# A state-space layer with a mixture of experts on one Trainium2 core: a new order for the first stage, with the third group's sine arguments made by GpSimd

## The chip, the cores and the metric

The kernel runs on one core of one Trainium2 chip. Its time is the device time of one launch, in microseconds. Five engines run their own instruction queues and meet at semaphores: TensorE (PE), VectorE (DVE), ScalarE (ACT), GpSimd (POOL) and SyncE (SP), which only issues DMAs. All data are float32.

## What is computed

```python
h = layernorm(x)                          # x: 2 x 2048 x 128
u = h @ in_W.T + in_b                     # along the sequence, per channel (128)
A = -exp(log_A_real) + 1j * A_imag        # 128 channels x 32 modes
K = exp(A * dt * arange(2048))
k = 2 * einsum('hn,hnl->hl', C * (exp(A * dt) - 1) / A, K).real
y = causal_convolution(u, k) + u * D_skip
y = gelu(y); z = y @ glu_W.T + glu_b; y = a * sigmoid(g)    # a, g: halves of z
x = x + (y @ out_W.T + out_b + h)
h = layernorm(x)                          # then 14 routed experts (top 2) and 2 shared ones
x = x + (moe(h) + h)
```

## The kernel before

The convolution is cut into 16 chunks of 128 positions per sequence. Within a chunk it is a product with a Toeplitz matrix of the first 128 values of k; from chunk to chunk a state of 32 complex modes per channel is carried. Both come from one table v1: for position s and mode n, exp(-|a|s) times sine and cosine of the mode's angle. The 128 channels are four groups of 32 (g = 0 to 3, 1024 columns each). This **first stage** is the span up to about 104 us; the gated unit, the routing and the loop over expert blocks follow and are the same in both kernels.

What the first stage does, and who does it:

- SP loads x, writes the small parameters `ab` to DRAM and reads them back broadcast to all partitions, one load of 1 MB a group (`abb[g]`, L394; groups 0 and 1 in `area`, 2 and 3 in `xn`). Later it loads the Toeplitz matrices of each group (`hank[g]`, L412) once the impulse response of that group is stored (`kp_out`), and for groups 2 and 3 once all of v1 is there.
- PE turns x by 512 columns at a time (`turn_x`, eight units, banks 0 and 1), ScalarE copies the turned block (`evict_xnT`, L1025), PE projects it (`project_in`, L1282, banks 2 to 7, then 2 and 3 again), and VectorE evicts the result (`evict_u`, L698, four operations a unit). The eviction scales by the reversed reciprocal roots `rstdr`, which one small product puts into bank 0 and VectorE copies (`reversed_roots`, L676).
- `table_args(g)` (VectorE, L685 to L690, four operations of 128x1024) brings the angle to within half a turn: round by adding and taking away a large constant, subtract, and clear the sign for the cosine's argument. `magnitude(g)` (ScalarE, L1034) makes the exponentials, `sines(g)` (ScalarE, L1039 and L1040) sine and cosine. `products(g)` (VectorE, L361, two of 128x1024) multiplies them into v1.
- PE makes the chunk states `states(g)` (L1293, into bank g), transposes the tables `turn_tables(g)` (L1306), which ScalarE copies into v2 (`evict_v2`, L1059), and multiplies them into the impulse response, `impulse(g)` (L1319), which ScalarE copies into `ksb` and stores (`evict_k`, L1065 to L1069). `ksb` shares its memory with the turned x and is cleared by a GpSimd memset first (L550).
- GpSimd makes the small coefficients `q1` and `q2` in a chain of 128x32 operations (L502 to L547). PE spreads them into banks 6 and 7 (L1337 to L1340), from where ScalarE copies `lw` and VectorE `cbig` (L724).
- VectorE weighs the states (L744 to L746) and runs the recurrence over the chunks (L756 to L761). ScalarE and VectorE copy its results into `s_bd` (L1105, L769). PE multiplies u with the Toeplitz matrices (L1361), then reads the states (L1370), which closes the convolution.

The order on each engine is written out by hand, and every queue is strictly in order. Before the change VectorE runs: arguments 0 and 1, eight evictions, products 0, cbig, arguments 2, products 1, arguments 3, products 2, products 3. `link(...)` makes the next instruction wait for the one inside it.

## Time and profile before

| | us |
|---|---|
| median of 3 runs (lowest to highest) | 412.38 (411.79 to 412.67) |
| the profiled execution: device time | 412.95 |
| the profiled execution: span | 411.2 |
| busy in the span: PE / DVE / ACT / POOL | 281.8 / 222.1 / 167.3 / 174.6 |
| mean granted clock of TensorE | 0.876 |

The profile is one execution. Times in its rows count from the start of its span; 1.75 us of the device time lie around it. A row gives start, duration, engine, line of the kernel, operation, what is written <- what is read, the count, and in brackets how long the engine was idle before it and what ended that. A count of TensorE's records is twice that of its instructions here, since each float32 product leaves two.

### The profile page before, as it was taken

The page shows a single profiled execution, that of the slowest core. Times are in us where ns is not written, and L with a number is a line of the kernel's source. Part 1 is how long each engine was busy: PE and PEld are TensorE (multiplying, and loading weights), DVE is VectorE, ACT ScalarE, POOL GpSimd, SP SyncE. Part 2 cuts the span into 40 slices and gives each one's busy share as a digit, 9 for nine tenths or more (in the row PEclk, how much of TensorE's full clock was granted, in tenths as well). Part 3 has the DMA queues.
Part 4 walks back from the last instruction along what each step waited for, and adds up shares of the span by engine and source line. Part 5 has one row for each costly group of instructions (what it writes and reads, how often), then busy time and mean ns, then how long its engine had stood idle before and what let it go on. Part 6 is the DMA issues. An engine that isn't in the chain of part 4 may idle for free.

```text
span 411.2 us, 9224 instructions
## 1 busy us (share of the span) xinstructions
PE 281.8 (69%) x2810; PEld 248.4 (60%) x2810; DVE 222.1 (54%) x837; ACT 167.3 (41%) x339; POOL 174.6 (42%) x231
## 2 busy tenths in 40 slices
PE   1945765559666768556656499969797879779800
PEld 1944654558454646354556398969686869678700
DVE  7999977972376455735653041353434343434374
ACT  1466486756485335543541132432323233232300
POOL 2793000008006447445647300355565655646540
PEclk9995798969996598889857599999999998999965
DMA  6750089997000111011102132122222232222289
GB/s 172 254 239 0 17 232 262 266 328 194 0 2 32 33 40 47 32 33 47 40 32 66 60 78 54 33 74 73 72 65 73 63 78 66 77 68 72 65 305 307
DMA packets 54577, 41.67 MB, mean 101 GB/s; under 512 B 6248, under 2 KB 50941, under 8 KB 54033
## 3 DMA queue, kind: packets, MB, share of 16 engines
q1 hardware_dynamic: 47552, 31.60, 26.8%
q0 software_dynamic: 4544, 8.47, 6.5%
q10 hardware_dynamic: 2448, 1.20, 1.1%
q8 instruction: 17, 0.28, 0.3%
q14 instruction: 16, 0.12, 0.1%
HBM read 29.14 MB, written 13.02 MB: 103 GB/s over the span
## 4 chain that ended last, share of the span: by engine, by line
PE 25%; DVE 25%; another core or an unknown queue 16%; issue 12%; DVEq 7%; DMA 5%; ACT 5%; SPq 4%; ACTq 0%
PE bank L1493 4%; DVEq L960 4%; PE bank L1581 3%; PE bank L1592 3%; PE bank L1474 2%; DVE u L698 2%; PE bank L1370 2%; PE bank L1416 2%; DVE area L980 2%; DMA area<-kp_dram 2%; ACT v L1059 2%; PE bank L1293 2%; PE bank L1306 1%; DVE stats L649 1%
## 5 line engine op out<-in xcount | busy, mean ns | idle before, releaser
L588 POOL DMA_INDIRECT y_dram<-area,ybi x78 | 77.9, 998 | 87.8 <-DVE area L980 70.5
L582 POOL DMA_INDIRECT xs_dram<-area x64 | 63.0, 984 | 64.5 <-issue 39.3
L961 DVE COPY v<-v 128x512 f32 x84 | 37.1, 441 | 31.0 <-issue 31.0
L1581 PE MATMUL bank<-xn,v 128*128 128x128 f32 x320 | 44.6, 282 | 3.5 <-DVE v L961 1.8
L1592 PE MATMUL bank<-v,xn 128*128 128x128 f32 x312 | 42.6, 281 | 5.4 <-ACT xn L1240 5.4
L1581 PEld LDWEIGHTS bank<-xn,v 128*128 128x128 f32 x320 | 38.9, 192 | 7.6 <-DVE v L961 4.0
L1592 PEld LDWEIGHTS bank<-v,xn 128*128 128x128 f32 x312 | 38.8, 195 | 6.4 <-DVE area L980 5.2
L1240 ACT ACTIVATE xn<-bank 128x512 f32<-128x512 f32 x40 | 24.1, 602 | 33.0 <-PE bank L1581 20.1
L979 DVE COPY ybi<-area 128x2 uint32<-128x2 uint32 x39 | 7.0, 181 | 54.6 <-remote 40.0
L1235 ACT COPY xn<-bank 128x256 f32<-128x256 f32 x41 | 15.1, 371 | 45.5 <-remote 25.0
L1474 PE MATMUL bank<-v 128*128 128x128 f32 x160 | 26.5, 313 | 9.2 <-issue 9.2
L1474 PEld LDWEIGHTS bank<-v 128*128 128x128 f32 x160 | 24.0, 226 | 9.7 <-issue 9.7
L1150 ACT ACTIVATE area<-x_sb,shift,tbuf 128x128 f32<-128x128 f32 x32 | 13.2, 482 | 38.7 <-DVE shift L897 38.6
L1416 PE MATMUL bank<-wT,v 128*128 128x128 f32 x64 | 13.2, 370 | 22.2 <-DVE v L784 22.2
L1416 PEld LDWEIGHTS bank<-wT,v 128*128 128x128 f32 x64 | 11.1, 262 | 23.7 <-DVE v L784 23.7
L1572 PE MATMUL bank<-ident,area 128*128 128x128 f32 x82 | 15.9, 278 | 11.8 <-issue 8.5
L1572 PEld LDWEIGHTS bank<-ident,area 128*128 128x128 f32 x82 | 9.6, 142 | 13.9 <-issue 9.8
L564 POOL TENSOR_TENSOR x_sb<-x_sb,outb_bc 128x1024 f32<-128x1024 f32 x4 | 9.4, 2380 | 19.5 <-PE bank L1370 19.5
L980 DVE TENSOR_TENSOR area<-bank,area 128x256 f32<-128x256 f32 x39 | 16.3, 417 | 0.0
L552 POOL MEMSET cbig<- 128x128 f32 x1 | 0.2, 206 | 35.5 <-PE bank L1319 35.5
L862 DVE TENSOR_TENSOR u<-u,bank 128x112 f32<-128x112 f32 x8 | 2.2, 271 | 23.5 <-remote 22.7
L1282 PE MATMUL bank<-wT,xnT 128*128 128x128 f32 x64 | 11.0, 332 | 5.7 <-DVE u L698 5.7
(298 smaller groups left out, 641.6 us busy)
## 6 DMA issues: line engine op xcount, KB each, us to landing
area<-kp_dram SPq DMA_DIRECT2D x12, 512.0 KB, 6.8
area<-xs_dram SPq DMA_DIRECT2D x84, 65.0 KB
area<-y_dram SPq DMA_DIRECT2D x8, 512.0 KB, 7.6
x_sb<-in_L_attn_x SPq DMA_DIRECT2D x4, 512.0 KB, 8.0
area<-ab_dram SPq DMA_DIRECT2D x2, 1024.0 KB, 6.1
xn<-ab_dram SPq DMA_DIRECT2D x2, 1024.0 KB, 10.9
xn<-kp_dram SPq DMA_DIRECT2D x4, 512.0 KB, 6.8
out_x<-x_sb SPq DMA_DIRECT2D x8, 256.0 KB, 6.5
```

The costliest lines, as they stand in the source:

```text
L582: pool.indirect_dma_start(out=xs_dram.ap(), out_offset=bass.IndirectOffsetOnAxis(ap=pos[:, k, i:i + 1], axis=0), in_=hx[:, i, k, :], in_of ...
L588: pool.indirect_dma_start(out=y_dram.ap(), out_offset=bass.IndirectOffsetOnAxis(ap=ybi[:, z:z + 1].bitcast(U32), axis=0), in_=yb[:, z, :], ...
L960: r = dve.value_load(etab[0:1, bass.ds(at, 1)], min_val=0, max_val=(E - 1) * HID)
L961: v.tensor_copy(wc[:, z % STEP], v1_flat.rearrange("p (w m) -> p w m", w=2)[:, :, bass.ds(r, HID)]).then_inc(wc_ready, 1)
L980: v.tensor_tensor(yb[:, z:z + 2], bank[4 + p % 2][:, 0:2 * D].rearrange("p (j d) -> p j d", j=2), xs[:, row:row + 2, D + 1:D + 2].broadcas ...
L1240: a.activation(act_sb[:, p % 3], bank[2 + p % 2][:], ACT.Silu).then_inc(act_ready, 1)
L1416: last = mm(bank[4][:, P * q:P * q + P], aT[:, c % 2, P * q:P * q + P], wT[:, 3, :], start=True, stop=True)
L1474: last = mm(bank[in_bank(u_)][:, P * e:P * e + P], w1_sb[:, E + e // HC, P * (e % HC):P * (e % HC) + P], h0T[:, P * u_:P * u_ + P], start= ...
L1493: last = mm(bank[out_bank(u_)][:, out_at(u_):out_at(u_) + D], half[u_ % 3][:, e, :], w2h[:, e, :] if u_ < WOVEN else w2_sb[:, E + e // HC, ...
L1572: last = tr(bank[p % 2][:, P * j:P * j + P], xs[:, (2 * p + j) % UNROLL, 0:D], ident[:])
L1581: last = mm(bank[2 + p % 2][:, HID * j + P * c:HID * j + P * c + P], wc[:, (2 * p + j) % STEP, 1, P * c:P * c + P], xsT[:, p % 3, P * j:P ...
L1592: last = mm(bank[4 + p % 2][:, D * j:D * j + D], act_sb[:, p % 3, HID * j + P * c:HID * j + P * c + P], wc[:, (2 * p + j) % STEP, 0, P * c ...
```

## The change

It reorders the first stage, and GpSimd takes over the third group's arguments.

- **GpSimd**: behind the chain for q1 it makes the arguments of group 2, in seven operations of 128x1024 (five of one input, two of two) that use group 3's part of v1 as scratch. The cosine's argument is now the angle plus a quarter turn, brought to within half a turn again, so `sines(2)` takes a plain sine of it. The memset of `ksb` stands behind them.
- **VectorE**: no `table_args(2)` and no copy of the roots. Products 0 stand behind five evictions, the other three behind them; products 1 follow cbig, then arguments 3.
- **ScalarE**: magnitude 0 between the fifth and sixth copy of turned x, magnitude 1 before the last two; it copies the reversed roots. `evict_k(0)` stands before `sines(2)`, which waits for GpSimd. Most additions of x move behind `evict_k(3)`.
- **TensorE**: projections go round all eight banks, the q products use banks 2 and 3, the transposes of group 0 come before its states, and groups 1 to 3 all run states, transposes, impulse.

```diff
@@ -546,6 +548,20 @@
             tt(q1[:, 0, :], mag128[:], cs128[:], ALU.mult)
             link(tt(q1[:, 1, :], mag128[:], sn[:, 1, :], ALU.mult))
             g_.engine_nop().then_inc(q_ready, 1)
+            pool.wait_ge(abb_in[2], 16)
+            pool.wait_ge(mag_ready, 1)
+            pool.wait_ge(abb_used, 1)
+            turns = v1_flat[:, 6144:7168]
+            turns_h = turns.rearrange("p (h n) -> p h n", h=HG)
+            f = abb[2][:, :, N:2 * N]
+            link(ts(turns_h, f, srow[:, 0:1], MAGIC, ALU.mult, ALU.add))
+            ts(trig[2][:, 1].rearrange("p (h n) -> p h n", h=HG), f, srow[:, 0:1], None, ALU.mult)
+            link(ts(turns, turns, -MAGIC, None, ALU.add))
+            g_.engine_nop().then_inc(abb_used, 1)
+            link(tt(trig[2][:, 1], trig[2][:, 1], turns, ALU.subtract))
+            link(ts(turns, trig[2][:, 1], 0.25, MAGIC, ALU.add, ALU.add))
+            link(ts(turns, turns, -MAGIC, -0.25, ALU.add, ALU.add))
+            tt(trig[2][:, 0], trig[2][:, 1], turns, ALU.subtract).then_inc(pool_arg, 1)
             pool.wait_ge(u_ps, 8)
             g_.memset(ksb, 0.0).then_inc(ksb_zero, 1)
             pool.wait_ge(k_ps, NG)
@@ -671,14 +687,10 @@
                 v.scalar_tensor_tensor(out=nmr[:], in0=mv[:, :, 0], scalar=-1.0, in1=rstd[:],
                                        op0=ALU.mult, op1=ALU.mult).then_inc(scaled, 1)
 
-            def reversed_roots():
-                dve.wait_ge(rev_ps, 1)
-                link(v.tensor_copy(rstdr[:], bank[0][:, 0:NT]))
-
             def table_args(g):
                 dve.wait_ge(abb_in[g], 16)
-                if g >= 2:
-                    dve.wait_ge(mag_ready, g - 1)
+                if g == 3:
+                    dve.wait_ge(mag_ready, 2)
                 f = abb[g][:, :, N:2 * N]
                 rv = rnd.rearrange("p (h n) -> p h n", h=HG)
                 arg = trig[g][:, 1].rearrange("p (h n) -> p h n", h=HG)
@@ -695,7 +707,7 @@
 
                 dve.wait_ge(u_ps, i + 1)
                 for c in range(4):
-                    last = v.scalar_tensor_tensor(out=u[:, :, 4 * i + c], in0=bank[2 + i % 6][:, P * c:P * c + P],
+                    last = v.scalar_tensor_tensor(out=u[:, :, 4 * i + c], in0=bank[(i + 2) % 8][:, P * c:P * c + P],
                                                   scalar=rstdr[:, 4 * i + c:4 * i + c + 1], in1=inb_bc[:],
                                                   op0=ALU.mult, op1=ALU.add)
                 last.then_inc(u_ready, 1)
@@ -711,26 +723,27 @@
                 ln_stats(g)
             ln_scale()
             table_args(0)
-            reversed_roots()
             table_args(1)
             dve.wait_ge(b_in, 48)
-            for i in range(8):
+            dve.wait_ge(rev_ready, 1)
+            for i in range(5):
                 evict_u(i)
             products(0)
+            for i in range(5, 8):
+                evict_u(i)
 
             dve.wait_ge(q_ps, 1)
             for e in range(2):
                 dst = cbig[64 * e:64 * e + 64].rearrange("p (b i) m -> p b (i m)", i=4)
                 last = v.tensor_copy(dst[:, :, e:e + 10 * 3 + 1:10],
-                                     bank[7][0:64, e:P:2].rearrange("p (b i) -> p b i", i=4))
+                                     bank[3][0:64, e:P:2].rearrange("p (b i) -> p b i", i=4))
             last.then_inc(cbig_ready, 1)
-            table_args(2)
             products(1)
+            table_args(3)
             dve.wait_ge(lw_act, 1)
             v.tensor_scalar(lw[:, 2, :], lw[:, 1, :], -1.0, None, ALU.mult)
             v.tensor_scalar(lw[:, 4, :], lw[:, 3, :], -1.0, None, ALU.mult)
             link(v.tensor_scalar(lw[:, 5, :], lw[:, 5, :], -1.0, None, ALU.mult))
-            table_args(3)
             products(2)
             products(3)
 
@@ -1035,10 +1048,16 @@
                              scale=srow[:, 0:1]).then_inc(mag_ready, 1)
 
             def sines(g):
-                act.wait_ge(arg_ready, g + 1)
+                if g == 2:
+                    act.wait_ge(pool_arg, 1)
+                else:
+                    act.wait_ge(arg_ready, min(g + 1, 3))
                 a.activation(trig[g][:, 1], trig[g][:, 1], ACT.Sin, scale=TWO_PI)
-                a.activation(trig[g][:, 0], trig[g][:, 0], ACT.Sin, scale=-TWO_PI,
-                             bias=halfpi[:]).then_inc(trig_ready, 1)
+                if g == 2:
+                    a.activation(trig[g][:, 0], trig[g][:, 0], ACT.Sin, scale=TWO_PI).then_inc(trig_ready, 1)
+                else:
+                    a.activation(trig[g][:, 0], trig[g][:, 0], ACT.Sin, scale=-TWO_PI,
+                                 bias=halfpi[:]).then_inc(trig_ready, 1)
 
             for i in range(2):
                 evict_xnT(i)
@@ -1048,10 +1067,17 @@
             a.activation(sn[:], fr[:], ACT.Sin, scale=TWO_PI)
             a.activation(cs128[:], frq[:, 1, :], ACT.Sin, scale=-TWO_PI, bias=halfpi[:])
             a.activation(sh[:], fr[:, 0, :], ACT.Sin, scale=TWO_PI / 2).then_inc(psin_ready, 1)
-            for i in range(2, 8):
+            for i in range(2, 5):
                 evict_xnT(i)
-            for g in range(NG):
-                magnitude(g)
+            magnitude(0)
+            evict_xnT(5)
+            magnitude(1)
+            evict_xnT(6)
+            evict_xnT(7)
+            act.wait_ge(rev_ps, 1)
+            a.copy(rstdr[:], bank[1][:, 0:NT]).then_inc(rev_ready, 1)
+            magnitude(2)
+            magnitude(3)
 
             def evict_v2(g):
                 for i in range(4 * g, 4 * g + 4):
@@ -1077,26 +1103,26 @@
             sines(0)
             sines(1)
             act.wait_ge(q_ps, 1)
-            turned = bank[6][:, 0:P].rearrange("p (y q x) -> p y q x", y=2, q=2)
+            turned = bank[2][:, 0:P].rearrange("p (y q x) -> p y q x", y=2, q=2)
             a.copy(lw[:, 0:2, :], turned[:, :, 0])
             a.copy(lw[:, 3:6:2, :], turned[:, :, 1]).then_inc(lw_act, 1)
-            a.copy(rmsT[:], bank[6][:, P:P + EA]).then_inc(rms_ready, 1)
+            a.copy(rmsT[:], bank[2][:, P:P + EA]).then_inc(rms_ready, 1)
             evict_v2(0)
-            sines(2)
             act.wait_ge(dskip_in, 64)
             act.wait_ge(ksb_zero, 1)
             evict_k(0)
+            sines(2)
             evict_v2(1)
             sines(3)
             evict_k(1)
+            act.wait_ge(scaled, 1)
             evict_v2(2)
-            act.wait_ge(scaled, 1)
             add_norm(0, 2)
             evict_k(2)
-            add_norm(2, 14)
             evict_v2(3)
-            add_norm(14, 16)
+            add_norm(2, 4)
             evict_k(3)
+            add_norm(4, 16)
 
             def copy_states(ks, lo, hi):
                 for k in ks:
@@ -1276,16 +1302,20 @@
                 pe.wait_ge(xnT_ready, i + 1)
                 if i == 0:
                     pe.wait_ge(wT_ready, 1)
-                if i >= 6:
-                    pe.wait_ge(u_ready, i - 5)
+                if i == 7:
+                    pe.wait_ge(rev_ready, 1)
                 for c in range(4):
-                    last = mm(bank[2 + i % 6][:, P * c:P * c + P], xnT[:, i % 2, P * c:P * c + P], wT[:, 0, :],
+                    last = mm(bank[(i + 2) % 8][:, P * c:P * c + P], xnT[:, i % 2, P * c:P * c + P], wT[:, 0, :],
                               start=True, stop=True)
                 last.then_inc(u_ps, 1)
 
             def states(g):
                 pe.wait_ge(v1_dve, 2 * g + 2)
                 pe.wait_ge(u_ready, 8)
+                if g == 2:
+                    pe.wait_ge(rms_ready, 1)
+                if g == 3:
+                    pe.wait_ge(cbig_ready, 1)
                 for x_ in range(8):
                     for r in range(2):
                         for k in range(4):
@@ -1299,8 +1329,6 @@
                 for i in range(4 * g, 4 * g + 4):
                     if i >= 3:
                         pe.wait_ge(v2_act, i - 2)
-                    if i == 2:
-                        pe.wait_ge(rms_ready, 1)
                     for q in range(4):
                         p = 4 * i + q
                         last = tr(bank[4 + i % 3][:, P * q:P * q + P], v1[:, 2 * p:2 * p + 2].rearrange("p h r n -> p (h r n)"), ident[:])
@@ -1324,31 +1352,29 @@
             for i in range(8):
                 if i < 7:
                     turn_x(i + 1)
-                if i == 6:
-                    pe.wait_ge(xnT_ready, 7)
+                if i == 7:
+                    pe.wait_ge(xnT_ready, 8)
                     pe.wait_ge(scaled, 1)
-                    mm(bank[0][:, 0:NT], exch[:], rstd[:], start=True, stop=True).then_inc(rev_ps, 1)
+                    mm(bank[1][:, 0:NT], exch[:], rstd[:], start=True, stop=True).then_inc(rev_ps, 1)
                 project_in(i)
 
-            pe.wait_ge(u_ready, 8)
+            pe.wait_ge(u_ready, 2)
             pe.wait_ge(q_ready, 1)
             for c in range(4):
                 for k in range(4):
-                    mm(bank[6][32 * k:32 * k + 32, 32 * c:32 * c + 32], q1[:, c, :], ident[:, k:P:4], start=True, stop=True)
+                    mm(bank[2][32 * k:32 * k + 32, 32 * c:32 * c + 32], q1[:, c, :], ident[:, k:P:4], start=True, stop=True)
             pe.wait_ge(rms_in, 48)
-            tr(bank[6][:, P:P + EA], rmsn, ident[0:EA, 0:EA])
-            tr(bank[7][0:64, 0:P], q2[:].rearrange("p q n -> p (q n)"), ident[:]).then_inc(q_ps, 1)
-
-            for g in range(2):
+            tr(bank[2][:, P:P + EA], rmsn, ident[0:EA, 0:EA])
+            tr(bank[3][0:64, 0:P], q2[:].rearrange("p q n -> p (q n)"), ident[:]).then_inc(q_ps, 1)
+
+            pe.wait_ge(u_ready, 5)
+            turn_tables(0)
+            states(0)
+            impulse(0)
+            for g in range(1, NG):
                 states(g)
                 turn_tables(g)
                 impulse(g)
-            turn_tables(2)
-            impulse(2)
-            states(2)
-            states(3)
-            turn_tables(3)
-            impulse(3)
             pe.wait_ge(k_ready, NG)
             pe.wait_ge(v2_act, 16)
             pe.wait_ge(st_dve, NG)
```

(The two hunks left out declare the semaphores `rev_ready` and `pool_arg`.)

VectorE before, from the first eviction on. L698 is an eviction, L361 half of a group's products, L724 cbig, L685 to L690 the arguments, L730 to L732 small signs:

```order
L698 SCALAR_TENSOR_TENSOR u<-bank,rstdr,inb_bc 128x128 x32
L361 TENSOR_TENSOR v<-area 128x32x32 x2
L724 COPY cbig<-bank 64x16x4 x2
L685 TENSOR_SCALAR area<-xn,srow 128x1024
L686 TENSOR_SCALAR area<-area 128x1024
L687 SCALAR_TENSOR_TENSOR area<-xn,srow,area 128x1024
L690 TENSOR_SCALAR area<-area 128x1024
L692 ISA
L361 TENSOR_TENSOR v<-area 128x32x32 x2
L730 TENSOR_SCALAR lw<-lw 128x32
L731 TENSOR_SCALAR lw<-lw 128x32
```

and in the changed kernel, where L710 is the eviction, L363 the products, L738 cbig and L697 to L702 the arguments:

```order
L710 SCALAR_TENSOR_TENSOR u<-bank,rstdr,inb_bc 128x128 x20
L363 TENSOR_TENSOR v<-area 128x32x32 x2
L710 SCALAR_TENSOR_TENSOR u<-bank,rstdr,inb_bc 128x128 x12
L738 COPY cbig<-bank 64x16x4 x2
L363 TENSOR_TENSOR v<-area 128x32x32 x2
L697 TENSOR_SCALAR area<-xn,srow 128x1024
L698 TENSOR_SCALAR area<-area 128x1024
L699 SCALAR_TENSOR_TENSOR area<-xn,srow,area 128x1024
L702 TENSOR_SCALAR area<-area 128x1024
L704 ISA
L744 TENSOR_SCALAR lw<-lw 128x32
L745 TENSOR_SCALAR lw<-lw 128x32
```

The first products moved ahead of twelve of the 32 evictions, and of the two sets of arguments one is left, behind the second products.

GpSimd before, from the last coefficient on (L550 clears ksb):

```order
L547 TENSOR_TENSOR q<-mag,sn 128x32
L548 ISA
L550 MEMSET xnT 128x1024
L552 MEMSET cbig 128x128
```

and changed (L557 to L564 are the arguments, L566 clears ksb):

```order
L549 TENSOR_TENSOR q<-mag,sn 128x32
L550 ISA
L557 TENSOR_SCALAR v<-xn,srow 128x1024
L558 TENSOR_SCALAR area<-xn,srow 128x1024
L559 TENSOR_SCALAR v<-v 128x1024
L560 ISA
L561 TENSOR_TENSOR area<-area,v 128x1024
L562 TENSOR_SCALAR v<-area 128x1024
L563 TENSOR_SCALAR v<-v 128x1024
L564 TENSOR_TENSOR area<-area,v 128x1024
L566 MEMSET xnT 128x1024
```

Seven large operations now stand between the coefficients and the memset.

ScalarE before, from the copy of rmsT on. L1059 copies transposes, L1039 and L1040 are the sines of group 2, L1065 to L1069 the first impulse response:

```order
L1083 COPY rmsT<-bank 128x16
L1059 COPY v<-bank 128x512 x4
L1039 ACTIVATE area<-area 128x1024
L1040 ACTIVATE area<-area,halfpi 128x1024
L1065 COPY xnT<-bank 128x128
L1066 ACTIVATE xnT<-bank,dskip 128x1
```

and changed (L1085 copies, L1091 to L1095 the impulse response, L1055 and L1057 the sines):

```order
L1109 COPY rmsT<-bank 128x16
L1085 COPY v<-bank 128x512 x4
L1091 COPY xnT<-bank 128x128
L1092 ACTIVATE xnT<-bank,dskip 128x1
L1095 DMA kp_dram<-xnT 128x256
L1055 ACTIVATE area<-area 128x1024
L1057 ACTIVATE area<-area 128x1024
```

The impulse response with its store went ahead of the sines, and the next copies of transposes stand behind both.

## Rows read from the trace of the kernel before

**Rows 1.** Busy time by stretch: PE, PEld, DVE, ACT, POOL, then PEclk, DMA share, GB/s

```profile
30.00:38.00 8.00, 3.75 (x16) 3.49 (x16) 8.00 (x33) 6.73 (x7) 3.96 (x15) 0.50 0.00 0
```

**Rows 2.** The chain that ended last, 58 to 96 us: start, us, what

```profile
71.86 5.50 DMA kp_dram<-xnT
...
80.01 6.70 DMA area<-kp_dram
...
86.75 3.64 PE bank L1361 x64
```

**Rows 3.** Timeline around 87 us, ScalarE's copies of the recurrence's last results

```profile
87.21 2.29 ACT L1105 COPY s_bd<-st 32x448 f32<-32x448 f32 x4 [3.30 <-DVEq L764]
```

**Rows 4.** Timeline of VectorE, 22 to 47 us

```profile
23.88 1.35 DVE L687 SCALAR_TENSOR_TENSOR area<-area,srow 128x1024 f32<-128x1024 f32 x1
...
29.64 8.50 DVE L698 SCALAR_TENSOR_TENSOR u<-bank,rstdr,inb_bc 128x128 f32<-128x128 f32 x32
...
37.97 2.34 DVE L361 TENSOR_TENSOR v<-area 128x1024 f32<-128x1024 f32 x2
...
40.23 0.54 DVE L724 COPY cbig<-bank 64x64 f32<-64x64 f32 x2
...
42.32 1.28 DVE L687 SCALAR_TENSOR_TENSOR area<-xn,srow,area 128x1024 f32<-128x1024 f32 x1
...
44.25 2.36 DVE L361 TENSOR_TENSOR v<-area 128x1024 f32<-128x1024 f32 x2
```

**Rows 5.** Timeline of TensorE, 36 to 66 us

```profile
40.37 1.93 PE L1293 MATMUL bank<-u,v 128*32 128x32 f32 x128 [0.92 <-DVE v L361]
42.23 3.68 PE L1306 MATMUL bank<-ident,v 128*128 128x128 f32 x16
46.67 1.06 PE L1319 MATMUL bank<-v,cbig 128*8 128x128 f32 x32 [0.77 <-ACT v L1059]
47.55 1.30 PE L1293 MATMUL bank<-u,v 128*32 128x32 f32 x128
```

**Rows 6.** Timeline of ScalarE, 19 to 60 us

```profile
19.84 0.59 ACT L1025 COPY xnT<-bank 128x512 f32<-128x512 f32 x1 [1.20 <-PE bank L1272]
...
25.80 1.28 ACT L1034 ACT_TABLE_LOAD   x1
27.10 2.19 ACT L1034 ACTIVATE area<-area,srow 128x1024 f32<-128x1024 f32 x2
...
48.71 0.26 ACT L1066 ACTIVATE xnT<-bank,dskip 128x1 f32<-128x1 f32 x1
...
51.36 2.05 ACT L1059 COPY v<-bank 128x512 f32<-128x512 f32 x4 [2.39 <-PE bank L1306]
53.28 1.09 ACT L1039 ACTIVATE area<-area 128x1024 f32<-128x1024 f32 x1
```

**Rows 7.** The loads of the broadcast parameters: issues (duration ns, first and last start), then landing

```profile
L394 SPq DMA_DIRECT2D area<-ab_dram x2: 339/387/435, 14.8 to 15.2; - x2
L394 SPq DMA_DIRECT2D xn<-ab_dram x2: 432/446/460, 15.7 to 16.2; - x2
...
DMA to landing us min/median/max: 4.7/7.5/12.2
```

**Rows 8.** Timeline of GpSimd, 22 to 36 us

```profile
24.23 1.11 POOL L526 TENSOR_TENSOR tbuf<-tbuf 128x32 f32<-128x32 f32 x1
...
31.12 0.29 POOL L539 TENSOR_SCALAR q<-tbuf 128x32 f32<-128x32 f32 x1
...
33.09 0.26 POOL L547 TENSOR_TENSOR q<-mag,sn 128x32 f32<-128x32 f32 x1
34.82 0.95 POOL L550 MEMSET xnT<- 128x1024 f32 x1 [1.48 <-PE bank L1282]
```

**Rows 9.** Groups of GpSimd's instructions by line and shape: busy us, mean ns of one | idle before

```profile
L564 POOL TENSOR_TENSOR x_sb<-x_sb,outb_bc 128x1024 f32<-128x1024 f32 x4 | 9.4, 2380 | 19.5 <-PE bank L1370 19.5
...
L496 POOL MEMSET cbig<- 128x512 f32 x1 | 0.5, 525 | 0.0
```

2 lines of the change are left out of this document (added).

## The prediction

> **What bounds the kernel now.** I read the table by stages first: the edit touches only the first 104 us, and from 30 to 38 us VectorE is busy for all 8.00 us while TensorE is for 3.75, at 0.50 of its clock, the lower of its levels, 1.2 GHz [rows 1]. Then the chain of waits: this stage ends when TensorE can read the states, at 90.39 us. Straight before it stand the last 64 Toeplitz records (86.75 + 3.64), which waited for the last piece of the Toeplitz matrices (80.01 + 6.70 = 86.71), and before that the store of the fourth impulse response, issued at 71.86 [rows 2]. A second path ends just earlier: the recurrence on VectorE, whose last results ScalarE has copied at 89.50 [rows 3]. Both go back to the same root. So I went back in the timelines and looked for what sets the start of group 1's states on TensorE: VectorE's queue of table arguments, evictions and products [rows 4]. From there on each group is a fixed sequence.
>
> I call **T1** the end of products(1): 44.25 + 2.36 = 46.61 us now. TensorE begins group 1's states at 47.55, as impulse(0) drains (46.67 + 1.06 = 47.73) [rows 5].
>
> **The sum, on the profiled run's own clock** (span 411.2, device time 412.95; the median of the runs is 412.38, 0.57 below).
>
> *1. Magnitudes between ScalarE's copies.* ScalarE is idle for 1.20 us before each copy of turned x [rows 6]. The first abb group was issued at 14.8 and landed 4.7 later, at 19.5 us [rows 7], so after the fifth copy (19.84 + 0.59 = 20.43) [rows 6] ScalarE loads its table (1.28) and makes magnitude(0) (1.09, half of 2.19 [rows 6]): the sixth copy starts at 22.8, where it started 1.79 behind the fifth, at 21.63. TensorE follows each copy as before, the last copy ends near 26.0 and the reversed roots, now ScalarE's, stand in SBUF near 26.9. VectorE asks for them only at 29.4. The table load costs nothing new, there are two before and after. The sines start near 30.7 (the last abb group, issued at 16.2, lands 12.2 later at 28.4 [rows 7], magnitude 1.09, load 1.28); sines(0), 2.1 like the pair at 53.28 [rows 6], is done by 32.9, before VectorE asks at 34.7. All of it costs 0 as long as evictions and table arguments cover it; if it were uncovered, the bound is the 1.2 us by which a copy is late.
>
> *2. Banks.* Evictions now rotate over eight banks, so the last two projections follow the roots at once instead of waiting for evictions. Cost and gain 0: the 32 evictions stand in one row without a gap [rows 4], VectorE was never short of a bank. The q products wait for GpSimd's last small product, 33.09 + 0.26 = 33.35 [rows 8], and end well before cbig asks at 40.
>
> *3. VectorE without the third group.* Evictions start at 29.42 (the copy of the roots is gone, 0.22 us). Eight units take 8.50 us [rows 4], 1.06 each: five end at 29.42 + 5.31 = 34.73. Products(0) 2.34: 37.07, against 40.31 before. Three evictions 3.19: 40.26. Cbig 0.54: 40.8. Products(1) 2.34: **T1 = 43.15** if nothing else stands in the way. That is 46.61 - 43.15 = 3.46 earlier, just what table_args(2) took (40.77 to 44.25 [rows 4]). TensorE: transposes 3.68, states 1.93, impulse 1.06 [rows 5] behind 37.07 end at 43.7, so it would begin group 1 at 43.7 instead of 47.55: **3.8 us**.
>
> *4. What GpSimd takes on:* five one-input and two two-input operations of 128x1024, behind 33.4 us, and behind them the memset that evict_k(0) waits for (at 34.82 before [rows 8]). Two-input: 2.38 each, from its own addition of that size [rows 9]. One-input is not in the trace at that size. From below, 0.95, the memset of it; from above 2.42, a 0.29 start plus 992 elements at the addition's (2.38 - 0.25)/992. I take the memset's slope, (0.951 - 0.525)/512 = 0.83 ns an element, on the 0.29 of the small tensor_scalar [rows 8, 9]: **1.11 us**, since one operand is read as in no addition. Sum 5 x 1.11 + 2 x 2.38 + five handovers of 0.07 = 10.7 us: to 44.1 undisturbed, memset to 45.0. Apart from the rows: the Trainium skill, GPSIMD Engine Reference, section Engine selection, calls one-input work there roughly line-rate; the 1.03 cycles an element at 1.2 GHz of its section Performance versus the Vector engine would make 0.88 us of 1024 elements, an estimate, and this sum 1.1 us shorter; no row here shows it.
>
> *5. What the two engines do to each other.* A GpSimd product of 128x32 takes 0.25 us; at 24.23, under VectorE's 1.35 us operation with two SBUF inputs, one took 1.11 and ended 0.11 behind VectorE's end [rows 4, 8]. The 128x32 operations at 31 to 33 us, beside evictions (one input in PSUM), were not stretched. So the two don't share. The other direction shows only as 1.35 against 1.28 us for VectorE's same operation without GpSimd [rows 4]: 0.07 behind a GpSimd operation of 0.25. Behind one of 1.1 to 2.4 us the wait lies between 0.07 and the whole of it. I take the whole, less 0.15 of start-up that the 0.11 above shows to overlap. Step by step, with GpSimd's seven operations called a to g (d and g have two inputs): a runs 33.4 to 34.5, b to 35.7. Products(0) asks at 34.73, waits for b, first half to 36.7; c to 37.7; second half to 38.7. The two-input d goes under the evictions (38.7 to 41.0), e to 42.1. Evictions end 41.9, cbig 42.4. f holds to 43.3, first half of products(1) to 44.35; g, 2.24, to 46.6; second half to **47.65 = T1**. So T1 itself now opens group 1, at 47.7 against 47.55, and nothing is left of the 3.8 us.
> The same rule stands in the Trainium skill (SBUF — State Buffer, section Who interferes with whom): an exclusive lock, the second one fully blocked, also for a VectorE operation with two SBUF inputs against GpSimd's reads. It speaks against this change; the trace agrees for GpSimd's side (1.11), and for VectorE's no row shows its size.
>
> *6. ScalarE.* Chain done 46.6, memset 47.5, evict_k(0) to 48.1, sines(2) (2.1) to 50.2. Copies of group 1's transposes began at 51.36 [rows 6], so this is hidden with 1.2 us to spare. From there sines(3) (53.28 before [rows 6]), products(3), the fourth group: the same steps, a states group ahead of its transposes instead of behind, the sum of TensorE's work alike, and ScalarE's additions of x only move behind the store. So products(3), the recurrence and the last store come within 0.1 to 0.2 us of before.
> Evict_k(0) itself ends 0.8 us earlier than the 48.71 + 0.26 = 48.97 of before [rows 6], and with it go the first store and the first Toeplitz loads. The later stores queue among loads (the fourth took 5.50 us [rows 2]), so loads that begin earlier free them earlier; I give the last landing half of the 0.8, 0.4 us. Landing is the later path by 90.39 - 89.50 = 0.9, so all of the 0.4 shows.
> Behind 90 us nothing is changed and each step follows its predecessor. **Forecast 412.4 - 0.4 = 412.0 us.**
>
> **Rivals.**
> A, *VectorE hardly waits* (0.07 instead of the whole length; GpSimd alone does). For it: the only direct row is 0.07. Against: GpSimd's side is exclusive. Group 1 starts 3.8 us earlier, evict_k(0) (45.5) and sines(2) (47.7) keep up with copies at 47.5, both paths move together: 412.4 - 3.8 = **408.6**. Half holding gives 410.4, still this side.
> B, *GpSimd is late, slower.* Place: evict_k(0) and sines(2) on ScalarE, behind the memset and the chain, with group 1's copies queued behind them. It decides once the chain ends after 46.6 + 1.2 = 47.8, that is when a one-input operation costs over 0.24 us more than 1.11. Midway to the upper bound (1.76) the chain is 3.2 us longer, the stage 3.2 - 1.2 = 2.0 later, and some 0.6 us more where VectorE waits for the longer pieces: 412.4 + 2.6 = **415.0**. At 2.42 all through, 419.
> C, *covered anyway*: the gain is real to products(3), but the last loads, back to back, keep the end where it is: the chain's last DMA steps. Against: their start hangs on the stores, which move too. 412.4.
>
> **How the numbers follow.** Forecast 0.42, own range 410.7 to 413.6; A 0.30; B 0.22; C 0.06. The range 408.3 (A with the one-input price at its lower bound, which lets evict_k(0) go 0.8 us sooner) to 415.0 (B) leaves out B's far end and some of A, 0.2 together. Over 0.2% is 0.8 us, about what a measurement of this kernel can tell from no change. Faster: A and 0.16 of the forecast, 0.46. Same: 0.19 of it, C and 0.02 of B, 0.27. Slower: 0.20 of B and 0.07 of the forecast, 0.27.
>
> **What would show it.** In the changed profile: VectorE's product at 128x1024 has a mean well over 1.22 us in groups 0 and 1, or gaps before it, and T1 lies near 47.6; tensor_scalar on GpSimd at 1.1 us where VectorE evicts, more elsewhere; group 1's states at 47.7; copies of its transposes at 51.4; last landing near 86.3. Products of 1.22 and T1 at 43.2 mean A. ScalarE idle before evict_k(0) or sines(2) on GpSimd until after 51 means B. Gains at products(3) but a landing at 86.7 mean C. The forecast is wrong above all if the wait in step 5 is not the GpSimd operation's length.

## The result, and the profile after

| | before | changed |
|---|---|---|
| median, us (lowest to highest) | 412.36 (411.79 to 412.67) | 425.00 (424.28 to 428.15) |
| profiled execution: device time / span, us | 412.95 / 411.2 | 425.49 / 423.7 |
| busy: PE / DVE / ACT / POOL, us | 281.8 / 222.1 / 167.3 / 174.6 | 284.4 / 224.1 / 167.4 / 196.4 |
| mean granted clock | 0.876 | 0.856 |

The change is slower: ratio 1.032, interval 1.0279 to 1.0362. The forecast was 412.0 with a range to 415.0. GpSimd's busy time gives the first hint: it grew by 21.8 us, where step 4 of the prediction allowed 10.7. Ratios and intervals are taken from the faster executions of each kernel, and two of the profiles read below, of the repeated run and of the shared arguments, are of executions 1.6 to 1.7% slower than the fastest of their kernel.

**GpSimd** of the changed kernel, timeline. A row gives start, duration, engine, line and instruction. L557 to L564 are the new arguments, L566 clears `ksb`:

```profile
33.96 1.13 POOL L557 TENSOR_SCALAR v<-xn,srow 128x1024 f32<-128x1024 f32 x1 [0.21 <-POOL q L549]
35.19 4.74 POOL L558 TENSOR_SCALAR area<-xn,srow 128x1024 f32<-128x1024 f32 x1
39.91 2.77 POOL L559 TENSOR_SCALAR v<-v 128x1024 f32<-128x1024 f32 x1
42.79 2.74 POOL L561 TENSOR_TENSOR area<-area,v 128x1024 f32<-128x1024 f32 x1
45.62 3.96 POOL L562 TENSOR_SCALAR v<-area 128x1024 f32<-128x1024 f32 x1
49.66 3.94 POOL L563 TENSOR_SCALAR v<-v 128x1024 f32<-128x1024 f32 x1
53.69 2.34 POOL L564 TENSOR_TENSOR area<-area,v 128x1024 f32<-128x1024 f32 x1
55.96 0.95 POOL L566 MEMSET xnT<- 128x1024 f32 x1
```

The chain starts when it should (33.96) and ends at 53.69 + 2.34 = 56.0, where 46.6 was forecast. Only its first instruction costs what the forecast gave to all five of one input. They run one behind another with gaps of at most 0.11 us, so the time is in the instructions and not between them. Whether GpSimd's own work or VectorE beside it makes them long, the rows don't tell; the experiments do.

**VectorE**, timeline (L363 products, L697 to L702 the arguments of group 3):

```profile
34.76 2.54 DVE L363 TENSOR_TENSOR v<-area 128x1024 f32<-128x1024 f32 x2
...
40.95 2.36 DVE L363 TENSOR_TENSOR v<-area 128x1024 f32<-128x1024 f32 x2
43.23 2.85 DVE L697 TENSOR_SCALAR area<-xn,srow 128x1024 f32<-128x1024 f32 x1
46.11 1.41 DVE L698 TENSOR_SCALAR area<-area 128x1024 f32<-128x1024 f32 x1
47.55 1.28 DVE L699 SCALAR_TENSOR_TENSOR area<-xn,srow,area 128x1024 f32<-128x1024 f32 x1
48.87 1.25 DVE L702 TENSOR_SCALAR area<-area 128x1024 uint32<-128x1024 uint32 x1
...
60.12 2.36 DVE L363 TENSOR_TENSOR v<-area 128x1024 f32<-128x1024 f32 x2 [8.91 <-ACT area L1057]
```

T1, the end of products(1), is 40.95 + 2.36 = 43.31, against 46.61 before [rows 4]. VectorE's queue did become shorter by all of step 3's 3.46 us, less 0.16. Products(1) last 2.36, exactly as before. But products(2) then wait 8.91 us for ScalarE.

**ScalarE** and **TensorE**, timelines (L1091 copies the first impulse response, L1334 are transposes):

```profile
56.99 0.27 ACT L1091 COPY xnT<-bank 128x128 f32<-128x128 f32 x1 [15.28 <-POOL xnT L566]
```

```profile
48.48 2.02 PE L1334 MATMUL bank<-ident,v 128*128 128x128 f32 x11 [2.32 <-issue]
60.51 1.11 PE L1334 MATMUL bank<-ident,v 128*128 128x128 f32 x4 [10.01 <-ACT v L1085]
62.39 1.89 PE L1347 MATMUL bank<-v,cbig 128*8 128x128 f32 x32 [0.77 <-ACT v L1085]
...
68.62 0.87 PE L1323 MATMUL bank<-u,v 128*32 128x32 f32 x48 [3.27 <-issue]
69.42 3.68 PE L1334 MATMUL bank<-ident,v 128*128 128x128 f32 x16
```

ScalarE stands 15.28 us before evict_k(0), for the memset behind the chain. The copies of group 1's transposes are queued behind it and behind `sines(2)`. They begin at 59.90, where they began at 51.36 [rows 6]: **8.5 us** of the loss. TensorE waits 10.01 us for them. Its granted clock was 1.00 from 44 to 48 us, fell between 48 and 50, behind the stop of 2.32 us in the first row, so before the idle 10 us, and stayed at 0.50 (1.2 GHz) until 73. In the 13 us behind the start of group 1's copies it is 0.50 here and was 0.98 before (51 to 64 us). From those copies to the fourth store it was 71.86 - 51.36 = 20.5 us, now 82.11 - 59.90 = 22.2: **1.7 us** more. The lower clock is the larger part of what the rows show for it: impulse(1) takes 1.89 us where it took 1.06, and the 16 transposes behind the states of group 2 take 3.68, where the 16 at the like place before, group 3's, took 2.64. TensorE's two stops without a wait on the way are 0.8 us longer together as well (3.27 and 1.19 against 2.79 and 0.86). That is more than 1.7, and the order of the groups differs too, so how the 1.7 divides isn't shown.

The end of the stage in the chain of waits (start, us, what), to be held against [rows 2]:

```profile
82.11 5.42 DMA kp_dram<-xnT
...
91.65 6.78 DMA area<-kp_dram
98.47 3.64 PE bank L1387 x64
```

The store is 10.25 us later and as long as before. Its load is issued 11.6 us later (SP's queue, 4.12 us from the store's end to the last issue, against 80.01 - 71.86 - 5.50 = 2.65): **1.5 us**. Why SP takes longer isn't shown. TensorE reads the states at 102.11 instead of 90.39 (102.04 and 90.32 in its timeline, from which the stage ends below are taken). These 11.7 us (8.5 + 1.7 + 1.5) are nearly all of the 12.5 by which the span grew.

### The profile page after: what moved, and what is told of

The parts are those of the page before. It is cut to its first block, busy times and chain, and to the rows that moved or that the text cites. A ratio compares the mean times of both kernels' runs of the same rounds, so it can differ in the third digit from the quotient of the medians.

```text
span 423.7 us, 9227 instructions
## 1 busy us (share of the span) xinstructions
PE 284.4 (67%) x2810; PEld 250.6 (59%) x2810; DVE 224.1 (53%) x832; ACT 167.4 (39%) x340; POOL 196.4 (46%) x238
## 4 chain that ended last, share of the span: by engine, by line
PE 26%; DVE 16%; issue 13%; another core or an unknown queue 12%; POOL 10%; DVEq 7%; DMA 6%; ACT 4%; SPq 4%; ACTq 0%; POOLq 0%
DVEq L973 4%; PE bank L1519 4%; PE bank L1607 3%; PE bank L1500 3%; PE bank L1618 3%; DMA area<-y_dram 2%; PE bank L1396 2%; DMA area<-kp_dram 2%; DVE area L993 2%; PE bank L1442 1%; DMA kp_dram<-xnT 1%; PE bank L1334 1%; DVE stats L839 1%; DVE x_sb L827 1%
## 5 line engine op out<-in xcount | busy, mean ns | idle before, releaser
L1618 PE MATMUL bank<-v,xn 128*128 128x128 f32 x312 | 43.7, 285 | 5.8 <-ACT xn L1266 5.7
L1500 PE MATMUL bank<-v 128*128 128x128 f32 x160 | 24.8, 297 | 9.0 <-issue 9.0
L1442 PE MATMUL bank<-wT,v 128*128 128x128 f32 x64 | 13.9, 384 | 22.8 <-DVE v L797 22.8
L1500 PEld LDWEIGHTS bank<-v 128*128 128x128 f32 x160 | 22.0, 209 | 9.2 <-issue 9.2
L1334 PE MATMUL bank<-ident,v 128*128 128x128 f32 x64 | 12.8, 374 | 14.6 <-ACT v L1085 10.0
L1598 PE MATMUL bank<-ident,area 128*128 128x128 f32 x82 | 15.8, 277 | 6.5 <-issue 5.5
L1334 PEld LDWEIGHTS bank<-ident,v 128*128 128x128 f32 x64 | 10.7, 194 | 15.6 <-ACT v L1085 10.4
L1387 PE MATMUL bank<-area,u 128*32 128x128 f32 x192 | 9.2, 372 | 9.2 <-DMA area<-kp_dram 8.6
L363 DVE TENSOR_TENSOR v<-area 128x1024 f32<-128x1024 f32 x8 | 9.6, 1244 | 10.8 <-ACT area L1057 8.9
```

The source lines that it names most:

```text
L1334: last = tr(bank[4 + i % 3][:, P * q:P * q + P], v1[:, 2 * p:2 * p + 2].rearrange("p h r n -> p (h r n)"), ident[:])
L1442: last = mm(bank[4][:, P * q:P * q + P], aT[:, c % 2, P * q:P * q + P], wT[:, 3, :], start=True, stop=True)
L1500: last = mm(bank[in_bank(u_)][:, P * e:P * e + P], w1_sb[:, E + e // HC, P * (e % HC):P * (e % HC) + P], h0T[:, P * u_:P * u_ + P], start= ...
L1618: last = mm(bank[4 + p % 2][:, D * j:D * j + D], act_sb[:, p % 3, HID * j + P * c:HID * j + P * c + P], wc[:, (2 * p + j) % STEP, 0, P * c ...
```

## The experiments

Eleven kernels ran, one of them twice, in four sessions. Each session timed the kernel before beside them, so ratios compare within a session. Times don't compare between sessions: the medians of before were 418.0, 413.5, 347.0 and 348.3 us there. "Stage end" is TensorE's first reading of the states, in each run's profile. One kernel profiled in two sessions gave 89.14 and 90.93, so differences below about 2 us in it carry nothing.

The theories: **F**, the form of a GpSimd instruction (which operators it applies) sets its price, and the chain is long by itself. Against it, the exclusion stretches both engines. **P**, TensorE's new order costs too.

### The prices by themselves

The kernel before, with these at the start of GpSimd's queue, twice over, while little else runs, then four at 256 columns (the products wait for GpSimd's coefficients too, since the scratch lies in v1):

```diff
...
+            for _ in range(2):
+                link(ts(za, zb, 1.0, MAGIC, ALU.mult, ALU.add))
+                link(ts(za, zb, srow[:, 0:1], MAGIC, ALU.mult, ALU.add))
+                link(ts(za, zb, 0.25, None, ALU.add))
+                link(ts(za, zb, 0.5, None, ALU.mult))
+                link(ts(za, zb, 0.25, MAGIC, ALU.add, ALU.add))
+                link(tt(za, za, zb, ALU.subtract))
...
```

> The kernel before, with GpSimd's operations measured by themselves: two memsets and then, at 1024 columns twice and at 256 columns once, multiply+add, one operation alone, add+add, and a subtraction of two tensors, all ahead of its first coefficient, on memory that is free until the tables. Nothing is left out. Theory F (the form sets the price): 1.1 us for multiply+add, with an immediate or a per-partition scalar, 2.7 for one operation alone, 3.9 for add+add, 2.35 for two inputs, the same both times round. Rival L (VectorE's operations stretched them in the changed kernel): all one-input forms 1.1 to 1.2 here. The total time is 25 to 30 us above before's and tells nothing.

Measured: 436.59 us in one run. GpSimd's timeline, the first round and the four at 256 columns (L511 (mult, add), L512 add alone, L513 (add, add), L514 two inputs):

```profile
5.66 1.04 POOL L505 TENSOR_SCALAR v<-v 128x1024 f32<-128x1024 f32 x1
6.80 1.12 POOL L506 TENSOR_SCALAR v<-v,srow 128x1024 f32<-128x1024 f32 x1
8.00 2.81 POOL L507 TENSOR_SCALAR v<-v 128x1024 f32<-128x1024 f32 x1
10.90 2.77 POOL L508 TENSOR_SCALAR v<-v 128x1024 f32<-128x1024 f32 x1
13.76 3.64 POOL L509 TENSOR_SCALAR v<-v 128x1024 f32<-128x1024 f32 x1
17.48 2.36 POOL L510 TENSOR_TENSOR v<-v 128x1024 f32<-128x1024 f32 x1
...
34.45 0.72 POOL L511 TENSOR_SCALAR v<-v 128x256 f32<-128x256 f32 x1
35.26 1.60 POOL L512 TENSOR_SCALAR v<-v 128x256 f32<-128x256 f32 x1
36.95 2.04 POOL L513 TENSOR_SCALAR v<-v 128x256 f32<-128x256 f32 x1
39.07 0.73 POOL L514 TENSOR_TENSOR v<-v 128x256 f32<-128x256 f32 x1
```

F is shown. L505 to L509 all have one input and one output of the same size, and cost from 1.04 to 3.64 us. A multiply with an add is cheap, whether the scalar is a number or a column. One operator alone costs 2.8, two adds 3.6. The second round agrees within 0.2 us. The first three at 256 columns are no prices of their own: VectorE's table arguments ran beside them (one of 2.71 us from 32.20 on, so it was still running when L511 began at 34.45), and the kernel on the lock below shows what that costs. L514 ran beside evictions. With these prices the chain's own work is 1.12 + 2 x 2.79 + 2 x 3.64 + 2 x 2.36 = 18.7 us; waits beside VectorE are the other 3.0 of the 22.1 (33.96 to 56.03, of which 0.4 are handovers).

### The arguments back on VectorE

The changed kernel without GpSimd's chain: `table_args(2)` stands behind cbig on VectorE, with the sines of before. All else of the change stays.

```diff
...
-            tt(trig[2][:, 0], trig[2][:, 1], turns, ALU.subtract).then_inc(pool_arg, 1)
...
+            table_args(2)
             products(1)
             table_args(3)
```

> The changed kernel with the third group's arguments back on VectorE, where they stood (behind cbig), in their old form; everything else of the new order stays. Theory F: GpSimd's chain was the whole loss, so this is back at 412 us within 1 us, 13 us faster than the changed kernel; products(1) end near 46.7 and evict_k(0) near 45. Rival O (the new order of TensorE and ScalarE costs something itself): 414 us or more.

Measured: 416.76 us, ratio 0.9952 (0.9905 to 0.9999), T1 46.5, stage end 89.14, the last store at 69.62. Run again in the third session, it gave 345.45 us, ratio 1.0034 (0.9987 to 1.0081), T1 46.8, stage end 90.93:

> The same kernel as e1_vector_args, to settle whether it beats the kernel before (there 0.9952, interval 0.9905 to 0.9999). Theory F (GpSimd's long chain is the whole loss, the rest of the change is worth a little): ratio 0.993 to 0.998 again. If the rest of the change is worth nothing: within 0.2%.

The gain of the first run was not seen again: the 0.993 to 0.998 expected of the repeat lie outside its interval, so the rest of the change is worth nothing that shows. What both runs show is that without the chain on GpSimd the loss is gone: the stage ends at 89.14 and 90.93, against 90.32 before and 102.04 in the changed kernel.

### The quick forms, in the chain's place

Every instruction of one input as (mult, add), with a factor of 1; `0.25 + MAGIC` can't be had in one of these, so there are six:

```diff
...
-            link(ts(turns, turns, -MAGIC, None, ALU.add))
+            link(ts(turns, turns, 1.0, -MAGIC, ALU.mult, ALU.add))
...
-            link(ts(turns, trig[2][:, 1], 0.25, MAGIC, ALU.add, ALU.add))
-            link(ts(turns, turns, -MAGIC, -0.25, ALU.add, ALU.add))
+            link(ts(trig[2][:, 0], trig[2][:, 1], 1.0, 0.25, ALU.mult, ALU.add))
+            link(ts(turns, trig[2][:, 0], 1.0, MAGIC, ALU.mult, ALU.add))
+            link(ts(turns, turns, 1.0, -MAGIC, ALU.mult, ALU.add))
...
```

> The changed kernel with GpSimd's one-input operations all written as multiply+add (a factor 1.0 or an addend 0.0 put in), six of them instead of five, since the quarter turn and the rounding constant are added one after the other; the same values. Theory F: six at 1.13 and two at 2.4 with handovers, 12 us, the chain ends near 46.5 instead of 56.0, evict_k(0) near 48, and products(1) are still early: 412 us, or down to 410. Rival L (VectorE stretches GpSimd's work): the chain stays above 18 us and the kernel above 418.

Measured: 425.27 us, ratio 1.0128 (1.0033 to 1.0222), stage end 95.98. The chain now ends at 50.0, 6 us sooner (46.5 was expected), and the stage end is 6.1 us sooner. GpSimd's timeline and VectorE's, the two halves of products(1) one at a time:

```profile
39.52 2.37 POOL L561 TENSOR_TENSOR area<-area,v 128x1024 f32<-128x1024 f32 x1
41.98 1.89 POOL L562 TENSOR_SCALAR area<-area 128x1024 f32<-128x1024 f32 x1
```

```profile
41.16 1.81 DVE L363 TENSOR_TENSOR v<-area 128x1024 f32<-128x1024 f32 x1
...
42.90 2.05 DVE L363 TENSOR_TENSOR v<-area 128x1024 f32<-128x1024 f32 x1
...
47.89 3.25 DVE L700 SCALAR_TENSOR_TENSOR area<-xn,srow,area 128x1024 f32<-128x1024 f32 x1
```

Now products(1) are stretched, to 3.78 us in all against 2.36, and the operation of two inputs in the arguments is too, 3.25 against 1.28. The own work of the eight is 11.1 us by the prices above, the chain lasts 15.8 (34.17 to 50.0): the exclusion is real, and it costs GpSimd some 4 us here. In the changed kernel products(1) had not met it. Why, the kernel on the lock below tells.

### The memset ahead of the chain

```diff
+            pool.wait_ge(u_ps, 8)
+            g_.memset(ksb, 0.0).then_inc(ksb_zero, 1)
...
-            pool.wait_ge(u_ps, 8)
-            g_.memset(ksb, 0.0).then_inc(ksb_zero, 1)
```

> The changed kernel with the memset of ksb ahead of GpSimd's chain. Theory F: evict_k(0) is free at 43.9 instead of 57, its store and the first Toeplitz loads go 12 us earlier, but the sines of group 2 still wait for the chain to 57 us, so the rest moves by only the memset's 0.95 us plus the 0.6 of evict_k(0), and by what loads that no longer queue give: 2 to 5 us off 425. Rival: if the late first store alone made the loss (the loads being the end of the stage), most of the 12.6 us come back, to 415 or less.

Measured: 426.0 us, ratio 1.0185 (1.0087 to 1.0284), stage end 98.89, so 3.2 us of the 11.7 come back. The first store leaves at 44.35 instead of 57.58, but the wait only moves one place down ScalarE's queue, to the sines:

```profile
57.75 1.06 ACT L1055 ACTIVATE area<-area 128x1024 f32<-128x1024 f32 x1 [13.43 <-POOL area L566]
```

The chain has two consumers there. Freeing the first one helps little while group 1's copies stand behind the second.

### Both together, and TensorE's order

Quick forms and the memset first; then the same with TensorE's order of before for groups 2 and 3 (and the arguments on VectorE with either order, two pairs):

```diff
-            for g in range(1, NG):
-                states(g)
-                turn_tables(g)
-                impulse(g)
+            states(1)
+            turn_tables(1)
+            impulse(1)
+            turn_tables(2)
+            impulse(2)
+            states(2)
+            states(3)
+            turn_tables(3)
+            impulse(3)
```

> As e8 but with TensorE's new order. Theory P: the third store leaves 4 us or more later than in e8 (near 67), the states are read 1 to 3 us later than in e8. Rival: the same as e8 within 0.5 us.

> The changed kernel with all three repairs: GpSimd's one-input operations as multiply+add, the memset of ksb ahead of the chain, TensorE's old order for the last two groups. Theory F with P: the chain (16 us in e3, 4 us of them waiting for VectorE's turns) ends near 50.5, the first store leaves at 44.3, the second near 58, the third by 62; the states are read near 91 to 93: 0 to 3 us slower than before, 9 us or more faster than the changed kernel. Rival A of the prediction (the engines hardly hold each other up): the chain ends by 47 and it beats before.

> As e1, with the third group's arguments behind products(1) on VectorE; TensorE's new order stays. Products(1) end near 43.2 instead of 46.5, the second store leaves near 53.5 instead of 55.0, the third near 62 (theory P) with the stall still in states(2). Time between e1's and 1.5 us below it. Rival: if products(1) are what everything hangs on, the states are read 3 us earlier than in e1, at 86.

> As e1, with the third group's arguments on VectorE behind products(1) instead of ahead of them, and with TensorE's old order for the last two groups (transposes and impulse of group 2, then states 2 and 3, then transposes and impulse 3). In e1 the third store left at 63.9 us against 60.2 in the kernel before, although the first two were early: a 3.2 us stall for instructions fell into states(2), which stand ahead of the transposes there. Theory P (TensorE's new order of group 2 costs the third store): products(1) end near 43.2, the third store leaves by 59, and the states are read from 86 to 88.5 us instead of 90.3, 2 to 4 us or 0.5 to 1% faster than before. Rival: the stall moves along with the order and the third store stays at 62 or later; then no gain on e1.

> e1_vector_args with TensorE's order of the kernel before for groups 2 and 3. From the two pairs measured so far (stage end 90.84 against 89.66, and 93.38 against 91.99) the new order is worth 1.2 to 1.4 us in the stage: this kernel should be 0.2 to 0.4% slower than e1_vector_args on the same chip, with the third store earlier and the fourth later. If TensorE's new order costs, it is faster instead.

| kernel | T1, us | stage end, us | ratio (interval) |
|---|---|---|---|
| quick, memset first | 46.3 | 91.99 | one run, 412.57 us beside 413.54 |
| the same, old order | 45.4 | 93.38 | 1.0078 (1.0041 to 1.0116) |
| arguments on VectorE behind products(1) | 43.1 | 89.66 | 1.0008 (0.9964 to 1.0052) |
| the same, old order | 42.7 | 90.84 | 0.9956 (0.9917 to 0.9994) |
| arguments behind cbig, again | 46.8 | 90.93 | 1.0034 (0.9987 to 1.0081) |
| the same, old order | 46.5 | 89.83 | 1.0031 (0.9977 to 1.0086) |

P is not borne out: the old order ends the stage 1.4 and 1.2 us later in two pairs and 1.1 sooner in the third, and the timed ratios lean one way in the second pair and are alike in the third. With the 2 us that one kernel's profiles differ by, the order is worth nothing that shows. Quick forms with the memset first bring the stage end back to 91.99 and 93.38, from 102.04 (90.32 before). The one of them that was timed is still 0.8% slower than before.

The third row holds something else: its T1 is 3.4 us ahead of that of the arguments behind cbig (46.5 in their first profile), and the stage doesn't end sooner. Where the 3.4 us go, the last experiment tells. The fourth row's interval lies just below 1; that kernel wasn't run again, and the lean of the same size in the first run of the arguments behind cbig was gone in the second.

### The lock by itself

The kernel before, with 36 products on VectorE ahead of its statistics, each waiting for the one before, beside twelve GpSimd instructions on other memory:

```diff
...
+            for _ in range(3):
+                link(ts(za, zb, 1.0, MAGIC, ALU.mult, ALU.add))
+            for _ in range(3):
+                link(ts(za, zb, 0.25, None, ALU.add))
+            for _ in range(3):
+                link(ts(za, zb, 0.25, MAGIC, ALU.add, ALU.add))
+            for _ in range(3):
+                link(tt(za, za, zb, ALU.subtract))
...
+            for _ in range(36):
+                link(v.tensor_tensor(vc, vc, vd, ALU.mult))
...
```

> The kernel before, with 36 chained VectorE products of 128x1024 (two inputs in SBUF) put ahead of its statistics, beside GpSimd's forms on other memory: three (mult, add), three (add) alone, three (add, add), three two-input, in this order. Only the rows of the stretch are of interest, the time is some 40 us longer. Theory L (the lock hangs on the form): VectorE's 1.18 us product is stretched beside (mult, add) and beside two inputs, to 2 us and more, but not beside (add) alone and (add, add). Rival (the lock is the same for all forms, and the 2.36 of products(1) in the changed kernel was luck of timing): stretched beside all of them, by the GpSimd operation's length, 2.8 and 3.7 us. Second rival: GpSimd's own times are what gives way; then its rows are longer than the 1.04, 2.8, 3.7 and 2.4 it has alone.

GpSimd's timeline, one instruction of each form (L507 (mult, add), L509 add alone, L511 (add, add), L513 two inputs):

```profile
17.58 1.90 POOL L507 TENSOR_SCALAR v<-v 128x1024 f32<-128x1024 f32 x1
...
26.49 3.15 POOL L509 TENSOR_SCALAR v<-v 128x1024 f32<-128x1024 f32 x1
...
38.31 4.41 POOL L511 TENSOR_SCALAR v<-v 128x1024 f32<-128x1024 f32 x1
...
49.28 3.20 POOL L513 TENSOR_TENSOR v<-v 128x1024 f32<-128x1024 f32 x1
```

VectorE's products beside them:

```profile
18.61 1.94 DVE L727 TENSOR_TENSOR v<-v 128x1024 f32<-128x1024 f32 x1
...
27.05 1.94 DVE L727 TENSOR_TENSOR v<-v 128x1024 f32<-128x1024 f32 x1
...
38.01 1.22 DVE L727 TENSOR_TENSOR v<-v 128x1024 f32<-128x1024 f32 x1
39.27 1.94 DVE L727 TENSOR_TENSOR v<-v 128x1024 f32<-128x1024 f32 x1
...
50.31 3.25 DVE L727 TENSOR_TENSOR v<-v 128x1024 f32<-128x1024 f32 x1
```

Neither the theory (no stretch beside the slow forms) nor its first rival (stretch by the GpSimd instruction's length) holds. A product takes 1.22 us undisturbed. Beside GpSimd's instructions of one input, **each** of the nine, whatever its form, stretches exactly one product by 0.72 us (the first by 0.77): the one that starts next after it (39.27, behind 38.31). The products that follow during the same slow instruction run at 1.22. An instruction of two inputs stretches one by 2.02. GpSimd in turn waits for the product that is running: 1.90 against 1.04, 3.20 against 2.36.

For (mult, add) and two inputs this is step 5's rule: VectorE waits for what is left of GpSimd's instruction, less 0.15. L513 from 49.28 ends at 52.48, 2.17 behind the product's start at 50.31, and 2.02 is the stretch. For the slow forms it is not: L509 from 26.49 ends 2.59 behind the start of its product, which was stretched by 0.72. A slow form holds VectorE's product up at its start alone, for about as long as a quick one does.

The waits in the other kernels come out of this. Products(1) of the changed kernel began at 40.95, 1.04 behind L559's start, and met nothing. L697, beside the two-input L561 with 2.30 us left of it, takes 2.85 against 0.75 before: 2.10. L698, at the start of L562, takes 1.41 against 0.69: 0.72. With the quick forms the first half of products(1) met the last 0.73 us of the two-input L561 (0.59 longer), and the second half L562, which had got in between them, with 0.97 left (0.83 longer).

One more wait belongs to the slow forms. L702, an operation of one input on VectorE, takes 1.25 against 0.69 before. L562 began 3.25 us before it and had 0.71 left: 0.71 less 0.15 is the 0.56 by which L702 is longer. With the memset first, L697 began 0.74 us before the end of such an instruction and took 1.28 against 0.75. Two-input operations were not held there: products of the lock kernel ran at 1.22 with 0.6 us left of a single add. So VectorE's one-input operations can be held up a second time, in about the last microsecond of a slow form. Why at both ends and not in the middle is open.

What isn't explained is L558, which waited 1.97 us in the changed kernel, behind both halves of products(0); it did the same with the quick forms (3.01 against 1.04) and with the arguments shared. That the halves don't wait for each other, as the chained products here do, is not the reason: with the quick forms L562 got in between the halves of products(1), which don't either.

### The arguments shared

GpSimd makes the sine's argument in four instructions of quick forms and two inputs. VectorE clears the sign for the cosine's, one operation of 0.69 us:

```diff
             products(1)
+            dve.wait_ge(pool_arg, 1)
+            v.tensor_scalar(trig[2][:, 0].bitcast(U32), trig[2][:, 1].bitcast(U32), 0x7FFFFFFF, None,
+                            ALU.bitwise_and).then_inc(arg_ready, 1)
             table_args(3)
```

> The changed kernel with the third group's arguments shared: GpSimd makes the sine's argument alone in its quick forms (three of (mult, add), one of two inputs), VectorE clears the sign for the cosine's argument behind products(1) (0.69 us), and the sine and cosine are those of before. From e6_prices and e11_lock: the chain is 1.13 + 1.04 + 1.04 + 2.36 us and a wait of up to 2.1 behind products(0), so it ends near 41.9 and the memset near 42.9, well ahead of evict_k(0)'s need; VectorE's products(1) wait for 0.7 to 2.0 us of it, T1 lies between 43.3 and 45.4, against 46.5 with all arguments on VectorE. Theory F with the lock's price per operation: stores 1 us or more ahead of e1_vector_args's, stage end 87 to 89, ratio to before 0.988 to 0.996. Rival (the stage's end hangs on loads and TensorE's issue stalls, not on T1): T1 earlier as said but the stage end 89 to 91 and the ratio 0.995 to 1.003. If GpSimd's chain is still the bound, ScalarE idles ahead of L1073 or the sines and the first store is later than 45.

Measured: 346.57 us, ratio 1.0015 (0.9940 to 1.0089), stage end 90.52. VectorE's timeline:

```profile
41.17 2.95 DVE L363 TENSOR_TENSOR v<-area 128x1024 f32<-128x1024 f32 x2
44.05 0.68 DVE L740 TENSOR_SCALAR area<-area 128x1024 uint32<-128x1024 uint32 x1
```

TensorE's, first here, then with all arguments behind cbig (first profile):

```profile
48.33 1.88 PE L1328 MATMUL bank<-ident,v 128*128 128x128 f32 x15 [2.04 <-issue]
...
57.17 0.87 PE L1317 MATMUL bank<-u,v 128*32 128x32 f32 x48 [4.29 <-issue]
...
68.93 0.82 PE L1341 MATMUL bank<-v,cbig 128*8 128x128 f32 x19 [1.48 <-issue]
...
90.52 3.04 PE L1390 MATMUL bank<-v,s_bd 128*64 128x128 f32 x48
```

```profile
47.80 3.75 PE L1315 MATMUL bank<-ident,v 128*128 128x128 f32 x16
...
57.28 0.63 PE L1304 MATMUL bank<-u,v 128*32 128x32 f32 x48 [3.19 <-issue]
```

The chain ends at 41.9, T1 is 44.1 as expected, 2.4 us ahead of the kernel with all arguments on VectorE, and yet the rival holds. Against that kernel's first profile, the first store leaves 1.0 us later (44.85 against 43.82), group 1's 1.2 sooner (53.43 against 54.65), group 2's 0.3 sooner (63.55 against 63.88), and group 3's 0.8 later (70.38 against 69.62).

The time won at T1 is spent in TensorE's stops, "issue" in the rows. Here TensorE stops at the first of group 1's transposes and goes on at 48.33; there it arrives later, doesn't stop, and has them run from 47.80. Group 1's copies begin at 48.91 and 49.25: of 2.4 us, 0.3 are left. In states(2) both stop and go on at the same time, 57.17 after 4.29 us and 57.28 after 3.19. The DMA rows show what stands before the end of each stop, a packet of 16 KB in the queue q8, whose kind is "instruction". In the window from 54.4 to 55.6 us of the shared kernel:

```profile
q8 instruction: 1, 0.02, 5.8%
```

| kernel | packet runs, us | TensorE goes on, us | stop, us |
|---|---|---|---|
| shared | 45.94 to 46.95 | 48.33 | 2.04 |
| shared | 54.47 to 55.58 | 57.17 | 4.29 |
| arguments behind cbig | 54.85 to 55.83 | 57.28 | 3.19 |
| arguments behind products(1) | 46.05 to 47.09 | 48.51 | 2.59 |
| arguments behind products(1) | 54.09 to 55.26 | 56.77 | 1.07 |
| before | 60.87 to 62.38 | 63.95 | 2.79 |
| changed | 65.97 to 67.12 | 68.62 | 3.27 |

In the profiles of all kernels but the two with measuring instructions put in, TensorE has 36 such stops of over 0.5 us between 40 and 90 us, and every one ends 1.2 to 1.6 us after a packet of q8 has landed. So TensorE most likely stands there for its own instructions. That is read from the agreement of the times; no run changed the packets. It also tells where the third row's 3.4 us went: the packet lands at 47.09 with T1 at 43.1 and at 47.08 with T1 at 46.5, and group 1's copies begin at 49.45 and 49.25. What sets the time of a packet is open. No version was shown to beat the kernel before.

## Why the prediction was wrong

- **Steps 1, 2, 3: right.** The sixth copy of turned x started at 22.67 (forecast 22.8), the roots stood at 26.65 (26.9), the evictions ran without a gap, and T1 was 43.31 where step 3 had 43.15 "if nothing else stands in the way".
- **Step 4 failed, and with it the forecast.** It gave 1.11 us to every one-input operation of 1024 columns. That is the right price for one of the five (1.13 measured) and wrong for four: 2.8 and 3.6. The five cost 14.0 us instead of 5.6, an error of 8.4 in a stage that lost 11.7. The kernel without the chain, back at the stage end of before, shows that this was the loss. The step took the memset's slope on the start of a small tensor_scalar. It held for sure that one input can't cost more than two ("from above 2.42"), so the range was no bound either. The trace of before had a warning in its small operations: at 128x32 a single operator takes 0.29 us [rows 8], more than the 0.26 of two inputs, and (mult, add), which I didn't look at, 0.22. Two forms of one instruction with two durations at one size say that the form must be priced. Of the Trainium skill, GPSIMD Engine Reference, section Engine selection, one-input work as roughly line-rate agrees with the (mult, add) at 1.04 us, and with none of the other forms.
- **Step 5 was half right.** The engines do exclude each other, and for (mult, add) and two inputs VectorE's wait is what the step said, the rest of GpSimd's instruction less 0.15 (0.72 and 2.02 measured). For the slow forms that ran it is not: the wait was 0.72 at their start, where the rule would give up to 2.7 and 3.5, and for a one-input operation of VectorE 0.56 at the end. T1 was 43.31, not 47.65, because products(1) fell into the middle of a slow form; that it met step 3's 43.15 is luck. With the quick forms, close to the step's own prices, T1 was 44.95, and the waits cost GpSimd some 4 us where the step had 2.5. The chain with its sixth instruction ended at 50.0, and the stage 5.7 us later than before: so a right price alone would hardly have made 412.0 right. The Trainium skill, SBUF — State Buffer, section Who interferes with whom, has two-input VectorE work contending with GpSimd's reads, and the runs agree. Its exclusive lock lasts for the whole instruction, and here it didn't for the slow forms: 1.22 us products ran beside one of 4.4.
- **Step 6 named the right place.** The slack of 1.2 us before ScalarE's queue binds was right: the chain's end came 9.4 us late, which less 1.2 is 8.2, and group 1's copies 8.5 us late.
- **Rival B was the mechanism**, in its place (evict_k(0) and `sines(2)` on ScalarE, group 1's copies behind them) and with its condition, a chain that ends after 47.8. It ended at 56.0. B's price stopped at 419 for 2.42 us all through; by its own rule 56.0 gives 412.4 + 8.2 = 420.6. The stage lost 3.5 us more than these 8.2: 0.3 before the copies, and the two terms that the rule lacked, 1.7 from the copies to the last store, where TensorE ran at its lower clock and stopped for longer, and 1.5 in SP's issues. The chance of 0.22 was too low because a price taken from no like row was treated as known to about 0.24 us, where B began.
- **Rival A** was right that T1 would be early, and wrong in what that is worth. Kernels with T1 from 42.7 to 44.1 and no late chain ended the stage at 89.7 to 90.8. Its 3.8 us don't reach the end. C put the place where they would be lost at the last loads; they were gone before that, in TensorE's stops.

## What to carry to other kernels

Price a GpSimd operation by its form, not by its count of inputs: rewriting a single add as (mult by 1, add) took it from 2.8 to 1.04 us here. Where work moves to another engine, price its longest instruction by a run of it alone before reasoning about what it hides behind, and look at the queue of whoever consumes the result: the memset and the arguments held one ScalarE queue, and moving one of them gave back 3 of 12 us. When work is taken off the engine that seemed to set the pace, check that the time arrives at the end: 2.4 to 3.4 us at T1 were spent in TensorE's stops a few microseconds on.

## What the hardware showed that was not expected

- GpSimd's tensor_scalar at 128x1024: 1.04 (mult, add), 2.8 (one operator), 3.6 (add, add), 2.36 for two inputs. At 128x32, in the trace of before, the first two are 0.22 and 0.29 and two inputs 0.25. So (mult, add) grows by 0.82 us over the 992 columns, a single operator by 2.5 and two inputs by 2.1, and no slope of one form serves another.
- Beside VectorE's products each one-input instruction of GpSimd costs VectorE 0.72 us once, whether it lasts 1 or 4 us. VectorE's one-input operations can be held up again near the end of a slow form (0.56 us, L702).
- TensorE's 36 stops without a wait between 40 and 90 us, 0.6 to 4.4 us long, all end 1.2 to 1.6 us after a 16 KB packet of the instruction queue q8 has landed.
- In the third and fourth session all kernels, the one before among them, were some 65 to 70 us faster (the kernel before 347.0 and 348.3, against 412.4 to 418.0 elsewhere). In the profiles of one kernel from two sessions (spans 413.6 and 347.6) the first 100 us are alike, and the loop over expert blocks is the shorter part: TensorE is busy 33.4 us of the 50 from 200 on in the one, 48.9 in the other. What sets this is open. Ratios are taken within a session, but the same microseconds are a larger share of 347 than of 412.
